# Layer 0 chunk by chunk: one pipeline of normalisation, scan output and router logits, column-tiled projections, and padding written during the dense experts

## The chip, the cores and the metric

One NeuronCore of a Trainium2 chip runs the whole program. The metric is the device time of one launch, in microseconds (us). The core has five engines with a queue each, all in order: TensorE (PE, with its weight loads shown as PEld), VectorE (DVE), ScalarE (ACT), GpSimd (POOL) and SyncE (SP), which here only issues DMAs. They wait for one another through semaphores, written `s_...` below.

## The reference, cut to what matters

Two layers over x of 16 sequences x 256 tokens x 128 features. Each layer has an adaptive layer norm with per-sequence scale and shift, an attention-like part, and a mixture of experts. The change touches layer 0 alone:

```python
h = layernorm(x) * (1 + ca) + sa
delta = sigmoid(h @ W_t.T + b_t) * 0.99 + 0.01      # one number per token
Bu = h @ W_b.T + b_b                                # 16 states per token
_, s = scan(exp(A * delta), Bu)                     # s[t] = a[t] * s[t-1] + Bu[t]
x = x + ga * ((s @ W_c.T + b_c + h * D) @ W_o.T + b_o)
h = layernorm(x) * (1 + cb) + sb
probs = softmax(h @ gate_weight.T)                  # 8 experts, the best two
expert_map = ...    # an expert that is nobody's first choice may be mapped to a similar one
combine = ...       # weight of each expert for each token, through expert_map
x = x + gb * sum_e combine[:, e] * (silu(g_e) * u_e) @ down_e.T    # g_e, u_e = h @ gate_up_e.T
```

Layer 1 (attention with relative positions, then routed experts whose tokens are dispatched by GpSimd) follows and is the same before and after.

## The kernel before

The 4096 tokens are 32 tiles of 128 and 8 chunks (`c`) of 512. `X` holds them in SBUF, `hT` the normalised features with features on partitions. Layer 0 runs as follows, each step in the in-order queues of the engines.

- **SP (from line 418)** loads the modulation weights, the 8 chunks of x, 12 small constants and the tables of layer 1. When the gates are computed (`s_gg`) it stores them and loads them back broadcast (`GATE`). Then it issues the padding: 8 pieces of 2064 KB and one of 903 KB, DRAM to DRAM, which fill the dispatch buffer that layer 1 uses far behind. After `s_yr` (all residuals done) it issues the router's tables (`gateT`, `sim`, `iota`) and the first two experts' weights. These go through the same queue as the padding.
- **Norm 0**: DVE computes `statistics(c)` for all chunks (4 bn_stats and 4 bn_aggr each), ACT one square root over all 32 tiles, DVE one reciprocal, then `normalise` writes `XN` chunk by chunk (4 operations each, double buffered). PE transposes a chunk (4 products with the identity), ACT applies scale and shift into `hT` (2 operations).
- **Projections**: for each half of 8 sequences, 8 products of 256 columns accumulate with the weights `WTpad`, and 8 with `WBpad`. Each is a full-width 128-column weight in which only 16 columns are not zero, shifted by 16 columns per sequence, so the 8 sequences' 16 states stack on the 128 partitions.
- **Scan**: ACT exp, DVE sigmoid and reciprocal, ACT exp, DVE scan, in two halves.
- **Outputs**: PE makes a chunk with 4 pairs of products (lines 1604 and 1605). DVE multiplies by the gate (`gated`, L1019), POOL adds it to X (L655), DVE makes the statistics of the chunk before. The bias row times the gate is added to X ahead of it, by DVE (L1039 and L1043).
- **Norm 1**: the same as norm 0, for all chunks, after all outputs.
- **Router**: PE makes the logits with `hT` as weights, 8 columns moving (L1612, 32 products). DVE and ACT make softmax and the two best of all 32 tiles, PE sums the first choices (L1620), DVE maps the experts, and the weights `WD` come out of a product over 8 x 32 x 8 elements and its reduction (L1140, L1143).
- **Dense experts** (`moe0`): 64 units, expert by expert and chunk by chunk. PE: two up products of 512 columns (L1638, L1639), ACT silu (L794), DVE times (`HM0`, L1170), PE 4 down products (L1627), DVE accumulates with the weight (L1152).

## Time and profile before

| what | us |
|---|---|
| median of 3 runs (lowest, highest) | 982.03 (975.97, 982.88) |
| the profiled execution | 988.27 |
| its span on the core | 986.4 |

Busy time in stages of the span, in us of 20 (granted TensorE clock as a share of full speed):

| stage | PE | DVE | ACT | clock | what runs |
|---|---|---|---|---|---|
| 0 to 20 | 8.40 | 16.63 | 3.12 | 1.00 | loads, statistics, gates |
| 20 to 40 | 15.12 | 17.68 | 9.32 | 1.00 | norm 0, projections; padding issued from 27.15 on |
| 40 to 60 | 16.28 | 13.46 | 3.28 | 0.91 | projections, scan, outputs |
| 60 to 80 | 13.60 | 18.64 | 6.01 | 0.78 | outputs, norm 1 |
| 80 to 100 | 11.82 | 0.53 | 3.67 | 0.59 | wait for a table, logits |
| 100 to 120 | 10.58 | 14.54 | 2.89 | 0.59 | router |
| 120 to 140 | 14.58 | 13.56 | 2.39 | 0.77 | expert weights, dense experts begin |
| 140 to 160 | 20.00 | 12.92 | 4.78 | 1.00 | dense experts |

### The profile page before, as it was taken

How to read it: one execution, taken by the hardware profiler on the slowest of the kernel's cores; microseconds unless marked ns; L12 is line 12 of the kernel's file. 1: busy time of each engine (PE TensorE's matmuls, PEld its weight loads, DVE VectorE, ACT ScalarE, POOL GpSimd, SP SyncE). 2: the span in 40 equal slices, each digit the busy share in tenths (PEclk: the TensorE clock that was granted, in tenths of full speed). 3: DMA queues.
4: the chain of work that ended last, by engine and by line, in shares of the span. 5: the costliest groups of instructions: out<-in, count | busy, mean ns of one | idle time of the engine just before them, and what ended most of it. 6: DMA issues, size and time to landing. Idle time of an engine off the chain costs nothing.

```text
span 986.4 us, 22653 instructions
## 1 busy us (share of the span) xinstructions
PE 837.8 (85%) x8752; PEld 581.6 (59%) x8752; DVE 608.9 (62%) x1652; ACT 354.6 (36%) x670; POOL 246.8 (25%) x248
## 2 busy tenths in 40 slices
PE   3876498999994979999999999998789889999960
PEld 3665355666663544666565665654456678888850
DVE  8882767666687888777877877865346322222218
ACT  1403112122224120563463463563545334444424
POOL 1040000000043640001211211214465624444440
PEclk9985589999997975999999999999799989999985
DMA  8995000000003673214423413312131437777746
GB/s 236 316 321 193 0 2 15 9 9 8 8 0 120 180 215 95 57 27 107 100 32 100 100 28 94 67 30 67 34 84 39 140 100 209 212 220 211 215 126 220
DMA packets 108820, 107.17 MB, mean 109 GB/s; under 512 B 50029, under 2 KB 95022, under 8 KB 108046
## 3 DMA queue, kind: packets, MB, share of 16 engines
q1 hardware_dynamic: 104190, 96.63, 34.9%
q0 software_dynamic: 4544, 9.35, 2.7%
q8 instruction: 60, 0.98, 0.4%
q14 instruction: 26, 0.21, 0.1%
HBM read 80.97 MB, written 44.77 MB: 127 GB/s over the span
## 4 chain that ended last, share of the span: by engine, by line
PE 57%; DVE 19%; issue 10%; SPq 5%; DMA 4%; ACT 2%; POOL 2%; POOLq 0%; DVEq 0%; another core or an unknown queue 0%; ACTq 0%
PE bank L2011 7%; PE bank L1791 7%; PE bank L2021 6%; PE bank L1627 5%; PE bank L1638 5%; PE bank L1639 5%; DVE sb_arena L1259 5%; PE bank L1731 4%; PE bank L1683 4%; PE bank L1709 3%; DMA sb_arena<-in_iota 2%; DVE sb_arena L1249 2%; DVE sb_arena L1251 2%; PE bank L1612 1%; PE bank L1593 1%
## 5 line engine op out<-in xcount | busy, mean ns | idle before, releaser
L1259 DVE TRANSPOSE_TENSOR_REDUCE sb_arena<-bank 128x16 f32<-128x512 f32 x192 | 120.3, 685 | 23.2 <-PE bank L1731 21.8
L837 ACT ACTIVATE sb_arena<-bank 128x512 f32<-128x512 f32 x192 | 99.2, 602 | 50.0 <-PE bank L1731 50.0
L925 ACT ACTIVATE sb_arena<-bank,sb_arena 128x256 f32<-128x256 f32 x156 | 65.3, 471 | 101.7 <-PE bank L2011 100.9
L741 POOL DMA_INDIRECT expert_results<-sb_arena x78 | 74.9, 960 | 94.1 <-DVE sb_arena L1518 77.8
L1627 PEld LDWEIGHTS bank<-sb_arena 128*128 128x128 f32 x512 | 67.5, 194 | 46.5 <-issue 25.7
L794 ACT ACTIVATE sb_arena<-bank 128x512 f32<-128x512 f32 x64 | 38.2, 598 | 152.4 <-PE bank L1639 152.4
L2011 PE MATMUL bank<-sb_arena 128*128 128x256 f32 x312 | 78.7, 396 | 4.6 <-DVE sb_arena L1514 2.1
L1627 PE MATMUL bank<-sb_arena 128*128 128x128 f32 x512 | 69.6, 280 | 14.8 <-DVE sb_arena L1170 14.8
L1791 PE MATMUL bank<-sb_arena 128*16 128x128 f32 x1024 | 72.9, 421 | 5.1 <-issue 4.8
L1170 DVE TENSOR_TENSOR sb_arena<-sb_arena,bank 128x512 f32<-128x512 f32 x64 | 43.7, 685 | 52.7 <-ACT sb_arena L794 52.4
L2021 PE MATMUL bank<-sb_arena 128*128 128x128 f32 x624 | 75.9, 275 | 0.0
L733 POOL DMA_INDIRECT dispatched_rows<-sb_arena x64 | 63.5, 992 | 45.7 <-issue 18.9
L1152 DVE SCALAR_TENSOR_TENSOR sb_arena<-bank,sb_arena 128x128 f32<-128x128 f32 x256 | 71.7, 343 | 3.0 <-PE bank L1627 3.0
L2021 PEld LDWEIGHTS bank<-sb_arena 128*128 128x128 f32 x624 | 72.8, 192 | 0.1
L1638 PE MATMUL bank<-sb_arena 128*128 128x512 f32 x128 | 69.0, 622 | 0.0
L1639 PE MATMUL bank<-sb_arena 128*128 128x512 f32 x128 | 67.5, 609 | 0.0
L2011 PEld LDWEIGHTS bank<-sb_arena 128*128 128x128 f32 x312 | 57.2, 193 | 16.5 <-issue 7.5
L1683 PE MATMUL bank<-sb_arena 128*128 128x56 bf16 (+1 forms) x512 | 62.2, 281 | 5.4 <-DVE sb_arena L1239 3.1
L1249 DVE CAST sb_arena<-bank 128x512 bf16<-128x512 f32 x64 | 43.6, 682 | 37.0 <-PE bank L1683 37.0
L1512 DVE CAST sb_arena<-sb_arena 128x2 uint32<-128x2 f32 x39 | 7.3, 186 | 94.7 <-DMA expert_results<-sb_arena 78.4
L667 POOL TENSOR_TENSOR sb_TMP<-sb_arena,sb_GATE 128x256 f32<-128x256 f32 x16 | 11.3, 726 | 214.4 <-DVE sb_arena L1152 214.3
L1731 PE MATMUL bank<-sb_arena,sb_identb 128*32 128x128 bf16 (+1 forms) x2304 | 62.4, 241 | 0.4 <-DVE sb_arena L1249 0.4
(252 smaller groups left out, 1395.4 us busy)
## 6 DMA issues: line engine op xcount, KB each, us to landing
sb_arena<-in_w SPq DMA_DIRECT2D x39, 578.0 KB
dispatched_rows<-in_padding SPq DMA_DIRECT2D x8, 2064.0 KB, 34.6
sb_arena<-dispatched_rows SPq DMA_DIRECT2D x39, 129.0 KB
sb_GATE<-gates SPq DMA_DIRECT2D x2, 2048.0 KB, 7.0
sb_arena<-q_parts SPq DMA_DIRECT2D x8, 512.0 KB, 5.7
sb_arena<-k_parts SPq DMA_DIRECT2D x8, 512.0 KB, 6.8
context_rel<-sb_arena SPq DMA_DIRECT2D x256, 8.0 KB
sb_arena<-expert_results SPq DMA_DIRECT2D x16, 256.0 KB, 5.8
```

Source lines behind the costliest of these rows:

```text
L741: nc.gpsimd.indirect_dma_start(yD[:, :], bass.IndirectOffsetOnAxis(ap=rid[:, k, r:r + 1], axis=0), YS[:, k, r, :], None).then_inc(s_yo[k], 16)
L837: nc.scalar.activation(dst, src, ACT.Exp).then_inc(s_ex, 1)
L1152: ins = v.scalar_tensor_tensor(out=ACC[:, T, :], in0=src[:, t * D:(t + 1) * D], scalar=wstep[:, (j // NC) % 2, T:T + 1], in1=ACC[:, T, :], ...
L1259: v.tensor_reduce(dst.rearrange("p h b -> p (h b)"), bank[r % RING][:, :].rearrange("p (b c) -> p b c", c=32), AX, ALU.max, apply_transpos ...
L1627: ins = mm(bank[4 + j % 2][:, t * D:(t + 1) * D], HM0[:, j % 2, t * P:(t + 1) * P], W0[:, k, 2 * F0:3 * F0], start=True, stop=True)
L1638: mm(bank[j % 2][:, :], W0[:, k, 0:F0], chunk(hT, c), start=True, stop=True)
L1639: mm(bank[2 + j % 2][:, :], W0[:, k, F0:2 * F0], chunk(hT, c), start=True, stop=True).then_inc(s_up[0], 1)
L1683: ins = mm(out[:, :, :, x], GT4[:, first:first + 32, :].rearrange("p x a -> p (x a)"), queries[:, :, :, q], start=True, stop=True, skip_gr ...
L1731: ins = mm(dst[32 * b:32 * b + 32, :, 32 * b:32 * b + w], identb[:, 32 * a:32 * a + 32], src[:, :, :].rearrange("p (g b) q -> p g b q", g= ...
L1791: ins = mm(out[32 * j:32 * j + 2 * HD, :, x], relk[:, 32 * j + 8 * w + 2 * x:32 * j + 8 * w + 2 * x + 2, :], four, start=True, stop=True, ...
L2011: ins = mm(bank[2 * (k % 2) + b // 2][:, b % 2 * GT:(b % 2 + 1) * GT], W1[:, k, b * P:(b + 1) * P], XT[:, k % 2, :], start=True, stop=True ...
L2021: ins = mm(bank[6 + k % 2][:, r * D:(r + 1) * D], HMT[:, k % 2, b, r * P:(r + 1) * P], W1[:, k, I1 + b * D:I1 + (b + 1) * D], start=(b == ...
```

## The change

- Norm 0 and norm 1 go chunk by chunk: `normalise0(n, c)` on DVE, `deviation` and `features0` on ACT, `transposes0` on PE. Statistics and normalisations of norm 0 alternate on DVE; the gates and masked matrices come after them.
- The 12 constants are one packed load; the loads of x are ordered around it. The router's tables and the first two experts' weights are loaded at the start, into memory of their own.
- Projections: weights of 32 columns, and four products to four groups of 32 output partitions (column tiles). 16 products a half as before.
- Outputs: the bias row is now a product of one row by 512 columns that opens each chunk's accumulation, and DVE's 16 products and 8 additions for it are gone. Behind outputs of chunk c, PE transposes chunk c-2 for norm 1, and DVE does gate product c, statistics c-1 and normalisation c-2.
- Logits: `gateT` (8 columns, widened to 32) is the weight, 512 columns move, four column tiles for four chunks; ACT copies them out and PE transposes them back. The router's DVE steps run on two halves of 16 tiles.
- The expert weights come from two one-hot comparisons over 256 elements each, not from the product over 2048.
- The first two `HM0` products are made ahead of the expert map.
- The padding is issued in pieces behind the experts' weight loads 2 to 7; the SP loop is written out.

```diff
+            for e in range(2, E):
+                sp.wait_ge(s_dn[0], (e - 1) * NC)
+                w0_load(e, e % 2)
+                padding(e - 2)
+                if e >= E - 2:
+                    padding(e)
...
+            def normalise0(n, c):
+                dve.wait_ge(s_sd, n * NC + c + 1)
+                ts = slice(c * TPC, (c + 1) * TPC)
+                link(v.reciprocal(RSTD[:, ts], SD[:, ts]))
+                wait(dve, s_tr, n * NC + c - 1)
+                for t in range(TPC):
+                    T = c * TPC + t
+                    ins = v.tensor_scalar(XN[:, c % 2, t, :], X[:, T, :], MV[:, T, 0:1], RSTD[:, T:T + 1],
+                                          ALU.subtract, ALU.mult)
+                ins.then_inc(s_xn, 1)
...
+            dve.wait_ge(s_gld, 16)
+            for c in range(NC + 2):
+                if c < NC:
+                    dve.wait_ge(s_y, c + 1)
+                    gated(c, bank[4 + c % 2][:, :].rearrange("p (b t f) -> p b t f", b=2, t=2), 0, 0)
+                if 1 <= c <= NC:
                     dve.wait_ge(s_yr, c)
                     statistics(c - 1)
-            dve.wait_ge(s_yr, NC)
-            statistics(NC - 1)
+                if c >= 2:
+                    normalise0(1, c - 2)
...
+            hidden0(0, 0)
+            hidden0(1, 1)
...
+            v.tensor_tensor(EQ[:, :, :], OH1[:, :, :], emaps, ALU.mult)
+            link(v.tensor_tensor(CD[:, :, :], OH2[:, :, :], emaps, ALU.mult))
+            v.tensor_reduce(id1[:, :], EQ[:, :, :], AX, ALU.add)
+            link(v.tensor_reduce(id2[:, :], CD[:, :, :], AX, ALU.add))
+            v.tensor_tensor(EQ[:, :, :], iota_t(NT), bc_e(id1[:, :]), ALU.is_equal)
+            link(v.tensor_tensor(CD[:, :, :], iota_t(NT), bc_e(id2[:, :]), ALU.is_equal))
+            v.tensor_tensor(EQ[:, :, :], EQ[:, :, :], bc_e(w1[:, :]), ALU.mult)
+            link(v.tensor_tensor(CD[:, :, :], CD[:, :, :], bc_e(w2[:, :]), ALU.mult))
+            link(v.tensor_tensor(WD[:, :, :].rearrange("p e t -> p t e"), EQ[:, :, :], CD[:, :, :], ALU.add))
...
+            def projections(h):
                 pe.wait_ge(s_hT, (h + 1) * NC // 2)
-                for pad, at in ((WTpad, S), (WBpad, 0)):
-                    for b in range(8):
-                        ins = mm(bank[2 + h][:, at:at + S], pad[:, 112 - N * b:240 - N * b],
-                                 hT[:, (8 * h + b) * S:(8 * h + b + 1) * S], start=(b == 0), stop=(b == 7))
+                for w, at in ((WT0, S), (WB, 0)):
+                    for x in range(2):
+                        for j in range(4):
+                            b = 8 * h + 2 * j + x
+                            ins = mm(bank[2 + h][32 * j:32 * j + 32, at:at + S], w[:, x, :], hT[:, b * S:(b + 1) * S],
+                                     start=(x == 0), stop=(x == 1), skip_group_check=True)
...
+            def logits0(g):
+                pe.wait_ge(s_hT, NC + 4 * g + 4)
+                for j in range(4):
+                    ins = mm(bank[2 + g][32 * j:32 * j + 32, :], gateT[:, :], chunk(hT, 4 * g + j), start=True, stop=True,
+                             skip_group_check=True)
+                ins.then_inc(s_lt, 1)
...
+            pe.wait_ge(s_zm, 1)
+            for c in range(NC):
+                outputs(c)
+                if c >= 2:
+                    transposes0(1, c - 2)
```

PE, from the last chunk of outputs to the router, before: L1604 and L1605 are the two products of a tile's output, L1580 the transposes, L1612 the logits.

```order
L1604 MATMUL bank<-sb_arena 128x128 [waits s_gt,s_hs]
...
L1605 MATMUL bank<-sb_arena 128x128
L1580 MATMUL bank<-sb_ident,sb_XN 128x128 [waits s_hT,s_xn]
L1580 MATMUL bank<-sb_ident,sb_XN 128x128 x3
...
L1612 MATMUL bank<-sb_arena 128x8 [waits s_hT,s_wm0]
```

PE in the changed kernel, chunk 3 and the beginning of chunk 4: L1663 is the bias row, L1669 and L1670 the output products, L1647 the transposes (of chunks 0 and 1 here).

```order
L1647 MATMUL bank<-sb_ident,sb_XN 128x128 [waits s_gg,s_hT,s_xn]
L1647 MATMUL bank<-sb_ident,sb_XN 128x128 x3
L1663 MATMUL bank<-sb_arena,sb_ones 128x512 [waits s_gt,s_hs]
L1669 MATMUL bank<-sb_arena 128x128
L1670 MATMUL bank<-sb_arena 128x128
...
L1647 MATMUL bank<-sb_ident,sb_XN 128x128 [waits s_hT,s_xn]
L1647 MATMUL bank<-sb_ident,sb_XN 128x128 x3
L1663 MATMUL bank<-sb_arena,sb_ones 128x512 [waits s_gt,s_hs]
```

The transposes, which stood in one block behind all outputs, now stand between the outputs of one chunk and of the next, with their wait for `XN`.

DVE in the outputs, before: L1019 is the gate product, L959 and L962 the statistics.

```order
L1019 TENSOR_TENSOR sb_TMP<-bank,sb_GATE 128x256 [waits s_yr,s_y]
L1019 TENSOR_TENSOR sb_TMP<-bank,sb_GATE 128x256
L959 BN_STATS sb_ST<-sb_X 128x6 [waits s_yr]
L959 BN_STATS sb_ST<-sb_X 128x6 x3
L962 BN_AGGR sb_MV<-sb_ST 128x2 [waits s_dv]
L962 BN_AGGR sb_MV<-sb_ST 128x2 x3
```

DVE in the changed kernel, the iteration of chunk 3: L1074 is the gate product, L985 and L988 the statistics of chunk 2, L997 and L1001 the normalisation of chunk 1; the last row is the gate product of chunk 4.

```order
L1074 TENSOR_TENSOR sb_TMP<-bank,sb_GATE 128x256 [waits s_yr,s_y]
L1074 TENSOR_TENSOR sb_TMP<-bank,sb_GATE 128x256
L985 BN_STATS sb_ST<-sb_X 128x6 [waits s_yr]
L985 BN_STATS sb_ST<-sb_X 128x6 x3
L988 BN_AGGR sb_MV<-sb_ST 128x2 [waits s_dv]
L988 BN_AGGR sb_MV<-sb_ST 128x2 x3
L997 RECIPROCAL sb_RSTD<-sb_SD 128x4 [waits s_sd]
L1001 TENSOR_SCALAR sb_XN<-sb_X,sb_MV,sb_RSTD 128x128 [waits s_tr,s_dv]
L1001 TENSOR_SCALAR sb_XN<-sb_X,sb_MV,sb_RSTD 128x128 x3
L1074 TENSOR_TENSOR sb_TMP<-bank,sb_GATE 128x256 [waits s_yr,s_y]
```

A reciprocal and four normalising operations have come in ahead of the next gate product.

## Rows read from the trace of the kernel before

**Rows 1.** Timeline, ACT and DVE: start, us, engine, line, out<-in, [idle before <-releaser].
```profile
82.67 1.28 ACT L786 ACT_TABLE_LOAD   x1
103.71 0.42 DVE L1084 TENSOR_REDUCE sb_arena<-bank 128x32 f32<-128x256 f32 x1 [23.19 <-PE bank L1612]
127.53 1.12 DVE L1152 SCALAR_TENSOR_TENSOR sb_arena<-bank,sb_arena 128x128 f32<-128x128 f32 x4 [1.57 <-PE bank L1627]
149.64 1.12 DVE L1152 SCALAR_TENSOR_TENSOR sb_arena<-bank,sb_arena 128x128 f32<-128x128 f32 x4
```

**Rows 2.** The chain of waits, 0 to 130: start us, us, what.
```profile
33.00 13.83 PE bank L1593 x64
70.22 19.52 DMA sb_arena<-in_iota
118.26 3.85 DVE sb_arena L1140
122.13 2.30 DVE sb_arena L1143
```

**Rows 3.** Timeline, from the start to the first output.
```profile
5.64 0.48 DVE L967 MEMSET bank<- 128x512 f32 x1 [0.18 <-DVE bank L967]
17.10 0.36 DVE L980 COPY sb_MOD<-bank 128x192 f32<-128x192 f32 x1
20.55 2.14 DVE L997 TENSOR_SCALAR sb_arena<-bank,sb_arena 128x128 f32<-128x128 f32 x8
47.37 0.30 DVE L1047 TENSOR_SCALAR sb_arena<-sb_arena 128x256 f32<-128x256 f32 x1 [2.50 <-ACT sb_arena L777]
49.37 0.39 DVE L1050 TENSOR_SCALAR sb_arena<-bank,sb_arena 128x256 f32<-128x256 f32 x1
50.53 0.71 PE L1604 MATMUL bank<-sb_arena 128*128 128x128 f32 x2 [3.72 <-DVE sb_arena L1052]
```

**Rows 4.** Timeline, DVE and PE while outputs run.
```profile
63.59 0.72 DVE L1019 TENSOR_TENSOR sb_TMP<-bank,sb_GATE 128x256 f32<-128x256 f32 x2
65.42 0.72 DVE L1019 TENSOR_TENSOR sb_TMP<-bank,sb_GATE 128x256 f32<-128x256 f32 x2
65.89 0.39 PE L1605 MATMUL bank<-sb_arena 128*128 128x128 f32 x2
66.11 0.39 PE L1604 MATMUL bank<-sb_arena 128*128 128x128 f32 x2
```

**Rows 5.** Timeline, transposes of one chunk, and DVE's last two chunks of norm 1.
```profile
31.32 0.66 PE L1580 MATMUL bank<-sb_ident,sb_XN 128*128 128x128 f32 x4 [0.59 <-DVE sb_XN L1007]
78.39 2.14 DVE L1007 TENSOR_SCALAR sb_XN<-sb_X,sb_MV,sb_RSTD 128x128 f32<-128x128 f32 x8 [0.18 <-PE bank L1580]
```

**Rows 6.** Timeline, PE, layer 1's column-tiled products (four of 256, then four of 128).
```profile
443.16 0.60 PE L1763 MATMUL bank<-sb_arena 128*9 128x256 f32 x8
443.59 0.39 PE L1767 MATMUL bank<-sb_arena 128*9 128x128 f32 x8
```

**Rows 7.** Timeline, PE, f32 products of 512 columns in the dense experts.
```profile
133.44 1.02 PE L1638 MATMUL bank<-sb_arena 128*128 128x512 f32 x2
134.30 1.02 PE L1639 MATMUL bank<-sb_arena 128*128 128x512 f32 x2
...
136.05 1.02 PE L1638 MATMUL bank<-sb_arena 128*128 128x512 f32 x2
```

**Rows 8.** Stages, PE: stretch, us, busy (records), granted clock, DMA share, GB/s.
```profile
50.00:52.00 2.00, 1.47 (x7) 0.66 0.66 220
...
78.00:80.00 2.00, 1.82 (x8) 0.50 1.03 352
80.00:82.00 2.00, 1.60 (x8) 0.66 1.06 352
```

**Rows 9.** DMA issues, 0 to 120 and 110 to 310: count, KB each, us to landing.
```profile
sb_arena<-in_w SPq DMA_DIRECT2D x2, 192.0 KB, 18.7
...
sb_arena<-in_w SPq DMA_DIRECT2D x6, 192.0 KB, 2.3
```

## Prediction: what the change does to the time, and why

> **What bounds the kernel now.** I read the 20 us stages first, then the chain of waits of the first 130 us, then the timelines of PE and DVE in it. From the dense experts on, the program stays as it is; what is changed lies ahead of the first weighted sum of an expert, at 127.53 [rows 1]. Up to there one engine after another works alone. The reader should see three long pieces in the chain [rows 2]: 13.83 us of scan projections on PE, 19.52 us until the last small router table lands behind the padding, and two big DVE operations of 3.85 and 2.30 us that make the expert weights. After 127.53 PE is the bound, at 2.61 us a unit (133.44 to 136.05) [rows 7]; the eighth accumulation later starts at 149.64 [rows 1]. So the sum is made for that instant: whatever the changed kernel has gained or lost there is its gain or loss. The padding has to be complete only for the dispatch, far behind.
>
> **Start until the first scan output.** Before, DVE makes all statistics, then everything else, and the first output product starts at 50.53 [rows 3]. Now DVE interleaves statistics and normalisation, and its own work is the bound: clearing the banks until 6.1, eight statistics of 1.19 (1.83 for gate product and statistics together, less 0.64 for the product) [rows 3, 4] = 9.5; eight normalisations of 1.07 [rows 5] and 0.3 for a reciprocal and its wait (a value that I choose, as the operand is eight times smaller than before) = 11.0; modulations and gate arithmetic 3.45; the masked matrices 2.14, with the widened bias row, the cast and the product M2 about 1.2 more; two sigmoids of 2.0; shift and scan 1.16 [rows 3]. That is 38.6; I take 39.0 for small waits. The two halves of projections go from 16 products in a row to groups of four column tiles. PE then has the second half ready at about 31, long before DVE asks at 34.5. The nearest rows are the attention's column tiles: four f32 products of 256 columns take 0.43 us together [rows 6], so a half costs 1.7 instead of 6.9. The worst case is that they do not overlap: 6.9 a half, which ends the second half near 41 and puts the outputs at 47 to 48. I take the overlap, since the row is of the same width and type. **Gain 11.5.**
>
> The Trainium skill (TensorE: Matmul & The Clock Gate, Part 3) says that a weight load overlaps running products only when the row group differs, and gives 2.38 times for three column tiles. By it the two halves would cost about 6 us (an estimate), still hidden under DVE's work, and the sum would not move by more than a microsecond.
>
> **The output pipeline, where I expect most of the gain to go.** Before, outputs, gate products and statistics run freely, and all normalisations follow; the last one ends at 80.53 [rows 5], 30.0 after the first output. Now look at the two orders in the section on the change. PE does outputs(c), then the transposes of chunk c-2, then outputs(c+1). Those transposes wait for DVE's normalisation of chunk c-2, which stands last in DVE's iteration c; and DVE's iteration c+1 begins with the gate product, which waits for outputs(c+1). So from chunk 3 on, the two engines alternate: five periods, each the DVE part plus the PE part. DVE: 0.64 + 1.19 + 0.3 + 1.07 = 3.2. PE at the high clock: transposes 0.46 (four, from the 0.66 that includes the drain [rows 5]), the bias row as one product of 512 columns 0.86 [rows 7], eight products of 0.22 = 1.77 [rows 4], and 0.2 until DVE sees it: 3.3. At the low clock about twice that, 6.5. A product with one input row is not shorter, as time goes with the moving columns; nothing in the rows gives a reason to price it lower.
>
> Outside the five periods stand three outputs (2.8 + 2.6 + 2.6, high), one DVE part of 3.2 and a tail on DVE of one statistics and two normalisations, 3.9. High throughout: 8.0 + 3.2 + 5 x 6.5 + 3.9 = 47.6. Low throughout, 24.3 of PE work more: 71.9. Which clock? Before the outputs of the old kernel PE idled 3.72 us [rows 3] and the granted clock was at its low level when they began (0.66 in the stage 50 to 52, where 0.50 is 1.2 GHz and 1.00 is 2.4 GHz) [rows 8]. In the new loop every burst follows 3.2 us of idleness, close to that. Once low, a burst lasts 6.3 us, of which the second half is full products; they may bring the clock back, and the next idle stretch takes it away. I take half of the PE work low: 47.6 + 12.2 = 59.8. **Loss 59.8 - 30.0 = 29.8.**
>
> **From the last normalisation to the router.** Before: 80.53 to 103.71 [rows 1, 5], 23.2 us: transposes, the wait for the table [rows 2], 32 products whose moving side has 8 columns. The tables are now loaded at the start and the padding leaves the queue, so nothing lands late. After the last normalisation there remain: transposes 0.9, features about 1.0, four column tiles of 512 columns 0.9 to 1.7, a copy 0.6, the table load 1.28 [rows 1] and an exponential 0.3, some 5.9; the low half's shift is done by then. **Gain 17.3.**
>
> **The router and the weights.** Before, 23.8 from 103.71 to 127.53 [rows 1]. Now the same steps run on two halves of the tiles. An operation of 256 elements takes 0.42 and 0.04 to the next; of 128 elements I take 0.33 in all (an eighth of a microsecond fewer columns; the fixed part stays). Behind the first exponential: 8 + 2 + 7 + 8 + 7 operations of 0.33 = 10.6, the count 0.55, five small ones 1.0, the two hidden products that moved ahead 1.3, twelve small ones of the expert map 3.0, nine operations of 0.42 to 0.46 in place of the two big ones = 4.0, the copy 0.2: 20.7. **Gain 3.1.** Splitting gains little, since most of an operation's time is fixed; the gain is 6.15 less 4.0, and that PE's first product is no longer waited for.
>
> **The lead of two units.** The first two hidden products now run before the expert map, so PE has two down products and two further up products done when DVE starts to accumulate: 2 x 2.61 = 5.2, less the 1.9 that PE then waits for DVE's first turns, less some 1.3 for PE starting this stage low as before. **Gain 2.0.**
>
> **Padding in the experts.** 16.5 MB leave the stretch 27 to 90 and go out one or two pieces behind each weight load, when before only the weights were in flight. A weight load behind the padding landed after 18.7 us, alone after 2.3 [rows 9]. Now each weight load is issued ahead of its padding, 21 us before it is needed, and the padding behind the previous one (nine pieces took some 60 us together until 89.74 [rows 2], so about 7 us a piece, at most two) is gone by then. Cost 0; if that cover failed, PE would wait up to 16 us once an expert.
>
> **Sum.** -11.5 + 29.8 - 17.3 - 3.1 - 2.0 = **-4.1 us**. The profiled execution took 988.27 us with a span of 986.4; the median of the three runs is 982.03. I subtract from the median: **978**.
>
> **Rivals.**
> - *The clock stays high in the loop* (idle stretches of 3.2 are a little shorter than the 3.72 that went low): 12.2 less, -16.3, **966**. Chance 0.17.
> - *The clock stays low in the whole loop*: 12.2 more, +8.1, **990**, slower than before. For it: in the stage 78 to 80, PE was busy 1.82 of 2.00 with transposes and stayed at 0.50 [rows 8]; the loop's bursts begin with transposes and a product of one row. It decides for slower once more than two thirds of the loop's PE work is low. Chance 0.22. The Trainium skill (the same page, Part 4) states that transposes do not bring the clock up; here it rose within 80 to 82 (0.66) with nothing but transposes before it [rows 8], so the rule is not exact, but it points this way.
> - *The column tiles do not overlap*: the outputs start 8 later, 986. Chance 0.04.
> - *Padding disturbs the experts* (code loads or weights late at a loop's start): one to two microseconds an expert, 982 to 990. Chance 0.05.
> - *The forecast*, a mixed clock with the alternation: 970 to 986. Chance 0.52.
>
> **The numbers.** Range 966 to 990: it takes in both clock cases' centres and leaves about a fifth outside, for their far halves and the other rivals. About 1% is what a measurement of this kernel can tell from no change, 9.8 us. Faster by more: most of the high clock case and a small part of the mixed one, 0.23. Slower by more: the far end of the low case and of the padding case, 0.11. Within: 0.66.
>
> **What would show it.** In the changed kernel's timeline: the first output product near 39; then DVE gate products 6.5 apart at a high clock, up to 9.8 at a low one, with DVE idle behind PE's outputs and PE idle behind XN in turn. If the gate products come 3.5 apart, the alternation is wrong and the kernel is 15 to 20 us faster. The projections should take about 2 us a half, the logits no wait on a table, and the first accumulation should stand near 124 to 128 with the eighth later near 145. Weight loads that land after 2 to 3 us show that the padding costs nothing. If the stages behind the experts differ by more than two or three microseconds, I have overlooked something there.

## The result and the profile after

| | before | after |
|---|---|---|
| median of the runs beside each other | 980.48 us (4 runs, 975.97 to 982.88) | 986.63 us (4 runs, 984.55 to 995.11) |
| ratio after to before, 95% interval | | 1.0095 (1.0056 to 1.0133) |
| profiled execution, its span | 988.27, 986.4 us | 984.55, 982.7 us |

The change made the kernel about 1% slower; 4.1 us faster were forecast. Here and below, ratios leave out executions of the slow state (longer, at a lower clock), while the medians are of all executions. The two profiled executions stand the other way round: that of before was slow for its kernel, that of after the fastest of its four. So the spans can't be subtracted. What can be is an instant ahead of the part in which single executions differ (more on that at the end): the last weighted sum of the dense experts was at 301.32 before and is at 309.86 now, 8.5 us later, and 980.48 x 1.0095 is 9.3 us more.

The changed kernel in the 20 us stages (stretch, us, then busy us and records of PE, PEld, DVE, ACT and POOL, granted clock of PE, DMA share, GB/s):

```profile
40.00:60.00 20.00, 16.20 (x60) 10.91 (x60) 7.22 (x30) 1.89 (x4) 3.79 (x3) 0.69 0.46 176
60.00:80.00 20.00, 13.50 (x46) 8.97 (x44) 6.17 (x30) 2.41 (x6) 2.52 (x2) 0.67 0.00 1
80.00:100.00 20.00, 13.49 (x45) 9.41 (x44) 6.18 (x30) 2.41 (x6) 2.53 (x2) 0.50 0.00 0
100.00:120.00 20.00, 14.87 (x61) 8.53 (x60) 9.49 (x44) 7.21 (x14) 1.26 (x1) 0.69 0.00 1
```

From 60 to 100 PE is busy for 27 of 40 us and DVE for 12.35 of 40, together nearly the whole 40; the timeline below shows that they work in turn, not at the same time. The clock is at 0.50, its level of 1.2 GHz, for all of the third stage. One period of that loop, in the timelines of DVE and PE (start, us, engine and line, operation, output<-inputs, count; in brackets the idle time ahead of it and who ended it):

```profile
74.58 0.76 DVE L1074 TENSOR_TENSOR sb_TMP<-bank,sb_GATE 128x256 f32<-128x256 f32 x2 [6.79 <-PE bank L1670]
76.62 1.11 DVE L1001 TENSOR_SCALAR sb_XN<-sb_X,sb_MV,sb_RSTD 128x128 f32<-128x128 f32 x4
77.80 0.70 PE L1647 MATMUL bank<-sb_ident,sb_XN 128*128 128x128 f32 x4 [3.25 <-DVE sb_XN L1001]
78.42 2.07 PE L1663 MATMUL bank<-sb_arena,sb_ones 1*128 1x512 f32 x2
80.42 0.80 PE L1669 MATMUL bank<-sb_arena 128*128 128x128 f32 x2
...
84.25 0.76 DVE L1074 TENSOR_TENSOR sb_TMP<-bank,sb_GATE 128x256 f32<-128x256 f32 x2 [6.51 <-PE bank L1670]
...
94.33 0.76 DVE L1074 TENSOR_TENSOR sb_TMP<-bank,sb_GATE 128x256 f32<-128x256 f32 x2 [6.92 <-PE bank L1670]
...
104.41 0.76 DVE L1074 TENSOR_TENSOR sb_TMP<-bank,sb_GATE 128x256 f32<-128x256 f32 x2 [6.92 <-PE bank L1670]
```

PE idles 3.25 for DVE's XN, then DVE idles 6.5 to 6.9 for PE's products; gate products stand 9.7 to 10.1 apart. In that burst the bias row (1x512) takes 2.00 until the next product starts. Before, gate products stood 1.83 apart [rows 4].

The 0.67 of 60 to 80 does not mean that part of the products ran fast. In stretches of 2 us (same columns as the stages above):

```profile
62.00:64.00 2.00, 2.00 (x12) 2.00 (x11) 0.00 (x0) 0.00 (x0) 0.00 (x0) 0.50 0.00 0
64.00:66.00 2.00, 0.60 (x3) 0.30 (x2) 1.37 (x6) 0.00 (x0) 0.53 (x1) 0.84 0.00 0
66.00:68.00 2.00, 0.15 (x1) 0.15 (x2) 1.72 (x10) 1.20 (x3) 0.73 (x1) 1.00 0.00 0
68.00:70.00 2.00, 2.00 (x6) 0.92 (x5) 0.00 (x0) 0.00 (x0) 0.00 (x0) 0.51 0.00 0
```

PE's products end at 64.6 and its next burst starts at 67.85. The clock was high in just that pause, and low again for the products. The output products of all five bursts of the loop ran at the low clock, 0.43 apart where they stood 0.22 apart before.

The other pieces of the changed stretch, in the same view, and two rows of its DMA issues (count, KB each, median us to landing):

```profile
33.59 1.93 PE L1656 MATMUL bank<-sb_arena 128*32 128x256 f32 x32 [1.58 <-ACT sb_arena L772]
...
40.55 1.86 PE L1663 MATMUL bank<-sb_arena,sb_ones 1*128 1x512 f32 x2 [5.02 <-DVE sb_arena L1095]
...
110.09 1.12 DVE L1001 TENSOR_SCALAR sb_XN<-sb_X,sb_MV,sb_RSTD 128x128 f32<-128x128 f32 x4
...
117.44 0.28 DVE L1135 TENSOR_REDUCE sb_arena<-sb_arena 128x16 f32<-128x128 f32 x1 [4.22 <-ACT sb_arena L810]
...
137.48 1.13 DVE L1210 SCALAR_TENSOR_TENSOR sb_arena<-bank,sb_arena 128x128 f32<-128x128 f32 x4
...
158.13 1.12 DVE L1210 SCALAR_TENSOR_TENSOR sb_arena<-bank,sb_arena 128x128 f32<-128x128 f32 x4
...
309.86 1.09 DVE L1210 SCALAR_TENSOR_TENSOR sb_arena<-bank,sb_arena 128x128 f32<-128x128 f32 x4
...
dispatched_rows<-in_padding SPq DMA_DIRECT2D x8, 2064.0 KB, 10.2
...
sb_arena<-in_w SPq DMA_DIRECT2D x8, 192.0 KB, 2.4
```

With these rows the forecast's sum can be set against the trace, term by term (all in us):

| piece | forecast | before | after | difference |
|---|---|---|---|---|
| start to first output product | -11.5 | 50.53 | 40.55 | -10.0 |
| first output to last XN | **+29.8** | 30.0 | 70.7 | **+40.7** |
| last XN to router (second half's exponential used) | -17.3 | 23.2 | 6.2 | -17.0 |
| router to first weighted sum | -3.1 | 23.8 | 20.0 | -3.8 |
| first to ninth weighted sum | -2.0 | 22.1 | 20.65 | -1.5 |
| sum | -4.1 | | | +8.4 |

One term missed. The four others are within 1.5 us each, and the padding, forecast at 0, is read from the two rows of the DMA issues: weights land after 2.4 us, and the experts take 172.4 us (137.48 to 309.86) against 173.8 before; the difference of 1.4 is that of the first nine (-1.5, the last row), and nothing is left for the padding.

### The profile page after: what moved, and what is told of

Read it like the earlier page. It is cut to its first block, busy times and chain, and to the rows that moved or that the text cites. A ratio compares the mean times of both kernels' runs of the same rounds, so it can differ in the third digit from the quotient of the medians.

```text
span 982.7 us, 22603 instructions
## 1 busy us (share of the span) xinstructions
PE 834.4 (85%) x8726; PEld 569.5 (58%) x8726; DVE 601.5 (61%) x1661; ACT 359.3 (37%) x687; POOL 246.3 (25%) x244
## 4 chain that ended last, share of the span: by engine, by line
PE 56%; DVE 20%; POOL 8%; DMA 6%; issue 6%; ACT 3%; SPq 2%; POOLq 0%; DVEq 0%
PE bank L2101 6%; PE bank L2111 6%; PE bank L1881 6%; POOL dispatched_rows L723 6%; PE bank L1715 5%; PE bank L1726 5%; PE bank L1727 5%; DVE sb_arena L1316 5%; PE bank L1821 4%; PE bank L1773 4%; PE bank L1799 3%; DMA dispatched_rows<-sb_arena 2%; DVE sb_arena L1306 2%; DMA expert_results<-sb_arena 2%; DVE sb_arena L1308 2%
## 5 line engine op out<-in xcount | busy, mean ns | idle before, releaser
L1316 DVE TRANSPOSE_TENSOR_REDUCE sb_arena<-bank 128x16 f32<-128x512 f32 x192 | 120.3, 684 | 23.8 <-PE bank L1821 22.3
L1881 PE MATMUL bank<-sb_arena 128*16 128x128 f32 x1024 | 68.4, 423 | 0.0
L1726 PE MATMUL bank<-sb_arena 128*128 128x512 f32 x128 | 67.6, 611 | 0.0
L1727 PE MATMUL bank<-sb_arena 128*128 128x512 f32 x128 | 65.7, 595 | 0.0
L1799 PE MATMUL bank<-sb_arena 32*128 32x256 bf16 x512 | 52.9, 285 | 6.5 <-DVE sb_arena L1316 4.5
```

The source lines that it names most:

```text
L1316: v.tensor_reduce(dst.rearrange("p h b -> p (h b)"), bank[r % RING][:, :].rearrange("p (b c) -> p b c", c=32), AX, ALU.max, apply_transpos ...
L1726: mm(bank[j % 2][:, :], W0[:, k, 0:F0], chunk(hT, c), start=True, stop=True)
L1727: mm(bank[2 + j % 2][:, :], W0[:, k, F0:2 * F0], chunk(hT, c), start=True, stop=True).then_inc(s_up[0], 1)
L1799: mm(dst[:, x * S:(x + 1) * S], KG[k][rows, g, 0:P], QG[k][rows, g, :], start=(x == 0), stop=False, skip_group_check=True)
L1881: ins = mm(out[32 * j:32 * j + 2 * HD, :, x], relk[:, 32 * j + 8 * w + 2 * x:32 * j + 8 * w + 2 * x + 2, :], four, start=True, stop=True, ...
```

## The experiments

Three theories of the 40.7 us were tested; they don't exclude one another. **A**: the place of the transposes in PE's order makes PE and DVE wait in turn. **B**: the bias row is a cost of its own. **C**: the clock is low because of something in that loop, and what that is. Every ratio is to the kernel before on the same chip, which took 980.4 us in e1 to e4, 1001.9 in e5 to e8 (another chip, on which the kernel before took 2% longer), and 980.2 in the last four (e9, e10, e11 and the changed kernel again). So times of different groups are compared by ratio. The changed kernel again, beside e9, e10 and e11, the second run of e1:

> The changed kernel itself once more, on the same chip as the other kernels of this call, so that they can be set against it directly. As before: ratio to the kernel before 1.006 to 1.013, last normalisation ending near 111, first accumulation near 137.

It took 988.83 (8 runs), ratio 1.0091 (1.0059 to 1.0123), with the last XN ending at 108.9 and the first weighted sum at 135.57.

**e1: products ahead of the transposes.**

```diff
             for c in range(NC):
                 outputs(c)
-                if c >= 2:
-                    transposes0(1, c - 2)
+                if c >= 3:
+                    transposes0(1, c - 3)
+            transposes0(1, 5)
```

> The changed kernel, in which TensorE issues the transposes of chunk c-3 behind the outputs of chunk c, where it was those of chunk c-2; those of chunk 5 follow the loop. Nothing else is changed. In the changed kernel the gate products stand 9.7 to 10.1 us apart from chunk 3 on (6.8 of PE, then 3.15 of DVE). Theory A (PE and DVE wait for each other in turn): the outputs of the next chunk now run while DVE normalises, so a period is the longer of the two and not their sum. With the clock still low it is some 6.8 us, 16 to 20 us less in all, 967 to 971 against the 986.6 of the changed kernel; with PE busy without a pause the clock may rise as well, a period is then DVE's 3.2 to 3.6, and the time 950 to 958. Theory B (the order costs nothing; the stage is long because one bias row and twelve other PE instructions a chunk at a low clock are that long): period unchanged, 984 to 988.

The median is 952.46 us, the ratio 0.970 (0.9669 to 0.9731). That is theory A, with both of its parts: the waiting in turn is gone and the clock is up. DVE in the loop:

```profile
62.29 0.76 DVE L1074 TENSOR_TENSOR sb_TMP<-bank,sb_GATE 128x256 f32<-128x256 f32 x2 [0.71 <-PE bank L1670]
...
65.75 0.76 DVE L1074 TENSOR_TENSOR sb_TMP<-bank,sb_GATE 128x256 f32<-128x256 f32 x2 [0.31 <-PE bank L1670]
...
69.23 0.75 DVE L1074 TENSOR_TENSOR sb_TMP<-bank,sb_GATE 128x256 f32<-128x256 f32 x2 [0.31 <-PE bank L1670]
...
105.21 1.12 DVE L1210 SCALAR_TENSOR_TENSOR sb_arena<-bank,sb_arena 128x128 f32<-128x128 f32 x4
```

DVE waits 0.3 us where it waited 6.9, the period is 3.47, and the first weighted sum comes 32 us earlier than in the changed kernel. One place in the order of one engine is worth 3.9% of the time, the difference between 1.0095 and 0.970. Once more, on the chip of the last group:

> The kernel of e1 once more on the same chip as the changed kernel and the candidate. As before: ratio to the kernel before 0.967 to 0.973, and to the changed kernel 0.958 to 0.964, which is the price of one line's order in the program (transposes of c-2 instead of c-3).

The median is 951.42, the ratio 0.9713 (0.9669 to 0.9757), and 0.962 of the changed kernel's 988.83.

**e2: the second normalisation behind all outputs again** (its loops on DVE, PE and ACT follow the output loop; the deviations stay one to a chunk).

```diff
             for c in range(NC):
                 outputs(c)
-                if c >= 2:
-                    transposes0(1, c - 2)
+            for c in range(6):
+                transposes0(1, c)
...
-                if c >= 2:
-                    normalise0(1, c - 2)
+            for c in range(NC):
+                normalise0(1, c)
```

> The changed kernel with one part undone: the second normalisation again stands behind all eight outputs on DVE and PE (the deviations stay one to a chunk, the logits stay as changed). Theory A: without the alternation the outputs run at 2.6 us a chunk as before the change plus 0.9 to 2.0 for the bias row, 28 to 37 us for eight, then 11 us of normalisations; the last one ends at 80 to 89 where the changed kernel had 111.2, so 22 to 31 us less, 956 to 965. Theory B (the bias row and the low clock alone make the stage long): the outputs need 6.5 us a chunk here too, the normalisations come on top, and the time is within 3 us of the changed kernel's 986.6 or above.

The median is 959.15, the ratio 0.9798 (0.9755 to 0.9841). Theory A again: without the interleaving, all other parts of the change together gain 2%. But the stretch from the first output to the last XN is 42.9 us (41.12 to 84.06), and 30.0 before. The rows of DVE show why:

```profile
58.64 0.75 DVE L1074 TENSOR_TENSOR sb_TMP<-bank,sb_GATE 128x256 f32<-128x256 f32 x2 [1.08 <-PE bank L1670]
...
61.67 0.76 DVE L1074 TENSOR_TENSOR sb_TMP<-bank,sb_GATE 128x256 f32<-128x256 f32 x2 [1.09 <-PE bank L1670]
```

A chunk takes 3.03 at the high clock, with DVE waiting 1.09 for PE. Before, it was 1.83 without a wait: with the bias row PE is the bound.

**e5: e2 without the bias row.** The output bias of layer 0 is missing from its result.

```diff
-                mm(bank[4 + c % 2][:, :], ones[0:1, :], crow[0:1, :], start=True, stop=False, skip_group_check=True)
...
-                    mm(dst, HSC[:, b // 8, at:at + P], ZM[:, b % 8, :], start=False, stop=False, skip_group_check=True)
+                    mm(dst, HSC[:, b // 8, at:at + P], ZM[:, b % 8, :], start=True, stop=False, skip_group_check=True)
```

> The kernel of e2 (second normalisation behind the outputs, 959.2 us) without the bias row: the product of ones and the bias is left out, and with it the output bias of layer 0 is missing from the result. In e2 the gate products stood 3.03 us apart with the clock up (PE the bound: 1.05 for the bias row to the next product, eight products of 0.22, 0.2 more) and 5.6 apart in the first two chunks at the low clock; the kernel before had 1.83 (DVE the bound) and no such row. If the bias row is what the stage pays for, periods fall to 1.83 to 1.95 and the first two chunks by 2.0 each: 9 to 11 us less, 948 to 950. If it lies beside DVE's work, as a cover of 1.1 us of DVE waiting would suggest at first sight, 1 us less a chunk at most and the time is 955 to 959.

The median is 970.26, the ratio 0.9696 (0.9625 to 0.9767); e2 had 0.9798. The point estimates differ by 1.0%, 10 us, as theory B says, though the intervals overlap; the trace is clearer:

```profile
44.16 0.76 DVE L1074 TENSOR_TENSOR sb_TMP<-bank,sb_GATE 128x256 f32<-128x256 f32 x2 [2.60 <-PE bank L1669]
46.07 0.76 DVE L1074 TENSOR_TENSOR sb_TMP<-bank,sb_GATE 128x256 f32<-128x256 f32 x2 [1.16 <-PE bank L1669]
...
55.27 0.72 DVE L1074 TENSOR_TENSOR sb_TMP<-bank,sb_GATE 128x256 f32<-128x256 f32 x2
```

The period is DVE's 1.83 again, and the last XN ends at 70.35, 13.7 us ahead of e2. That is more than eight bias rows at the high clock cost beyond DVE's cover (8 x 1.20 = 9.6): the first two gate products stand 1.9 apart, and 5.6 in e2. PE starts at the low clock in both; here it is up when the second chunk's products begin (0.91 in 44 to 46), in e2 only at 52.

**e3: the idle stretch filled.**

```diff
                 if c >= 2:
+                    for x in range(2):
+                        mm(bank[7][:, :], M2[:, :], wmod[:, 0, 0:CH], start=True, stop=True)
                     transposes0(1, c - 2)
```

> The changed kernel with two products of 512 columns added into each idle stretch of PE in the output loop (behind the outputs of chunk c, ahead of the transposes that wait for DVE; their result is not used), so that PE is busy where it idled 3.15 us a period. It tells what the clock adds to the alternation. If the idle stretches are what keeps the clock low, the granted clock goes up, PE's burst falls from 6.8 to about 3.4, the period from 9.9 to 6.5, and the time by 15 to 20 us to 967 to 972. If the clock stays low whatever stands in the gap, the two products take 3.5 to 4.0 us, a little more than the idle time, and the time goes up by 2 to 6 us, to 989 to 993.

The median is 971.46, the ratio 0.9903 (0.9867 to 0.9939). A stage of PE's clock and two gate products:

```profile
80.00:100.00 20.00, 14.85 (x82) 7.92 (x80) 10.30 (x50) 6.20 (x15) 2.53 (x2) 1.00 0.00 1
...
69.35 0.76 DVE L1074 TENSOR_TENSOR sb_TMP<-bank,sb_GATE 128x256 f32<-128x256 f32 x2 [3.78 <-PE bank L1670]
...
76.29 0.76 DVE L1074 TENSOR_TENSOR sb_TMP<-bank,sb_GATE 128x256 f32<-128x256 f32 x2 [3.78 <-PE bank L1670]
```

With 12 products of no use added, the first weighted sum is at 122.22, 15 us ahead of the changed kernel's (the ratios make it 19). The clock is at 1.00 where it was at 0.50, and the period 6.94. The alternation is all there still, now at the high clock: this splits the loss. The stretch from first output to last XN is 55.9 here (41.08 to 96.98), 70.7 in the changed kernel, 38.6 in e1: some 15 us of the 40.7 are the clock, 17 the waiting in turn at the high clock, and the rest of about 9, which e1 has too, is put down to the bias rows and the low start; e10 below, which changes those, is back at 31.2.

**e4: the bias row in the idle stretch.**

```diff
+            def bias_row(c):
+                wait(pe, s_gt, c - 1)
+                mm(bank[4 + c % 2][:, :], ones[0:1, :], crow[0:1, :], start=True, stop=False, skip_group_check=True)
...
-                wait(pe, s_gt, c - 1)
-                mm(bank[4 + c % 2][:, :], ones[0:1, :], crow[0:1, :], start=True, stop=False, skip_group_check=True)
...
+            bias_row(0)
             for c in range(NC):
                 outputs(c)
+                if c < NC - 1:
+                    bias_row(c + 1)
                 if c >= 2:
                     transposes0(1, c - 2)
```

> The changed kernel with the bias row of chunk c+1 issued behind the outputs of chunk c, ahead of the transposes that wait for DVE: the alternation stays, but the one-row product of 512 columns (2.0 us at the low clock in the trace) lies in PE's idle time. By its own duration alone a period falls by 2.0, from 9.9 to 7.9, seven periods, 12 to 14 us less: 973 to 975. If PE's shorter idle stretch also lets the clock rise, up to 25 us less, 962. If the bias row is hidden already, no change: 985 to 988.

The median is 963.79, the ratio 0.9836 (0.9798 to 0.9873), a gain of more than the 12 to 14 us of the row's own duration:

```profile
58.06 0.76 DVE L1074 TENSOR_TENSOR sb_TMP<-bank,sb_GATE 128x256 f32<-128x256 f32 x2 [3.69 <-PE bank L1672]
...
65.84 0.76 DVE L1074 TENSOR_TENSOR sb_TMP<-bank,sb_GATE 128x256 f32<-128x256 f32 x2 [4.62 <-PE bank L1672]
...
80.28 0.76 DVE L1074 TENSOR_TENSOR sb_TMP<-bank,sb_GATE 128x256 f32<-128x256 f32 x2 [3.94 <-PE bank L1672]
...
60.00:80.00 20.00, 14.35 (x65) 12.32 (x64) 7.36 (x36) 3.62 (x9) 2.69 (x3) 0.69 0.00 1
```

Periods are 6.8 to 7.8 with the clock still mixed. The trace up to the first weighted sum accounts for 16.2 us (121.31 against 137.48); the ratios, 1.0095 and 0.9836, make 25. The other 9 lie behind the first weighted sum and are not explained.

**e9: the bias over 128 input rows.** What, other than idle time, holds the clock?

```diff
+            nc.gpsimd.memset(crow[:, :], 0.0).then_inc(s_set, 1)
...
+            dve.wait_ge(s_set, 2)
             v.tensor_tensor(crow[0:1, :].rearrange("p (t d) -> p t d", t=TPC),
...
-                mm(bank[4 + c % 2][:, :], ones[0:1, :], crow[0:1, :], start=True, stop=False, skip_group_check=True)
+                mm(bank[4 + c % 2][:, :], ones[:, :], crow[:, :], start=True, stop=False, skip_group_check=True)
```

> The changed kernel with its bias product over all 128 input rows in place of one (the bias in row 0, zeros in the others, set once at the start), the same 512 columns; nothing else. In e1, PE was busy 2.00 of 2.00 us from 42 to 52 and the granted clock stayed at 0.50; in e5, the same outputs without the one-row products, it rose within the first chunk (first gate product 3.6 us after the first output product, the second 1.9 later). If the one-row product is part of what keeps the clock low, the clock now rises in the later half of each burst: the first two chunks together 3 to 4 us shorter, the periods of 9.9 to 10.1 fall to 8.5 to 9.2, and the time by 8 to 11 us (976 to 979 where the kernel before has 980, a ratio to the kernel before of 0.995 to 0.999). If rows don't matter and only idle time does, every period stays at 9.7 to 10.1, and the ratio that of the changed kernel, 1.009.

The median is 970.15, the ratio 0.9884 (0.9831 to 0.9938). The same order, the same products and columns, one small memset more, and 18.7 us less than the changed kernel beside it (988.83). Up to the first weighted sum the two traces account for 13.5 of that (122.06 against 135.57); the rest lies behind it and is not explained. e1, stretches of 2 us:

```profile
44.00:46.00 2.00, 2.00 (x11) 2.00 (x11) 0.00 (x0) 0.00 (x0) 0.00 (x0) 0.50 0.00 0
46.00:48.00 2.00, 2.00 (x6) 0.92 (x4) 0.76 (x2) 0.00 (x0) 0.34 (x1) 0.50 1.48 462
48.00:50.00 2.00, 2.00 (x7) 1.35 (x7) 0.00 (x0) 0.00 (x0) 0.92 (x1) 0.50 0.00 0
50.00:52.00 2.00, 2.00 (x11) 2.00 (x10) 0.00 (x0) 0.00 (x0) 0.00 (x0) 0.50 0.00 0
```

e9, the same stretches, and two gate products of its loop:

```profile
44.00:46.00 2.00, 2.00 (x13) 1.76 (x13) 0.27 (x1) 0.00 (x0) 0.00 (x0) 0.81 0.18 66
46.00:48.00 2.00, 2.00 (x18) 1.76 (x16) 0.49 (x2) 0.00 (x0) 1.27 (x1) 1.00 1.48 462
...
73.66 0.76 DVE L1076 TENSOR_TENSOR sb_TMP<-bank,sb_GATE 128x256 f32<-128x256 f32 x2 [3.40 <-PE bank L1672]
...
80.22 0.76 DVE L1076 TENSOR_TENSOR sb_TMP<-bank,sb_GATE 128x256 f32<-128x256 f32 x2 [3.40 <-PE bank L1672]
```

Both start an output burst after 5.02 us of idleness, near 41. With the one-row product PE is busy without a gap and the clock is still at its low level at 52; with 128 rows it is up after 44.

This first burst alone would not settle it. The changed kernel's second trace has the one-row products and the same start, and its clock is up at 46:

```profile
46.00:48.00 2.00, 2.00 (x10) 1.12 (x10) 0.76 (x2) 0.00 (x0) 0.42 (x1) 0.97 1.28 462
...
46.74 0.76 DVE L1074 TENSOR_TENSOR sb_TMP<-bank,sb_GATE 128x256 f32<-128x256 f32 x2 [4.54 <-PE bank L1670]
...
49.70 0.76 DVE L1074 TENSOR_TENSOR sb_TMP<-bank,sb_GATE 128x256 f32<-128x256 f32 x2 [2.21 <-PE bank L1670]
```

From the first output product to the rise it took 10 to 11 us in the six other traces that start with a one-row product behind 5.02 us of idleness (the changed kernel, e1, e2, e3, e7, e11), 4.9 in this one, and under 4 in the two without one-row products (e5, e9). So the long low start goes with the one-row product in most executions, not in all.

In the loop the difference is plainer: e9's periods are 6.56 to 9.29 instead of 9.4 to 10.1 (both traces of the changed kernel), although PE idles 3.25 us in each, and the clock is 0.91 in 60 to 80 and 0.74 in 80 to 100, where the changed kernel beside it has 0.59 and 0.50. So the one-row product was counted too cheaply twice: 2.0 us for itself, and products behind it that stay at the low clock. It is not the only cause: e3 keeps the one-row product and has 1.00 in both stages, and e1 too gets there from its third chunk on and keeps it, as PE has hardly a pause there. Theory C holds in that form: full products in the gap or a full bias product lift the clock. What exactly the chip counts was not tested, nor whether a product of another length would do the same.

**e6: the start filled, and the load order.**

```diff
-            load_x(0)
             sp.dma_start(cT[:, :, :], A["cT"]).then_inc(s_cw, 16)
             sp.dma_start(wmod[:, :, :], A["wmod"]).then_inc(s_cw, 16)
+            load_x(0)
...
+                if c >= 2:
+                    bias_row(c)
...
+            for x in range(2):
+                mm(bank[7][:, :], ident[:, :], wmod[:, 0, 0:CH], start=True, stop=True)
             pe.wait_ge(s_zm, 1)
+            bias_row(0)
+            bias_row(1)
...
```

> The kernel of e1 (952.5 us) with three small edits: two products of 512 columns whose result is not used and the bias rows of chunks 0 and 1 are issued ahead of the wait for the first scan, where PE idled 5.02 us; and the modulation weights are loaded ahead of the first rows of x. If it is the idle stretch that makes the outputs begin at the low clock, the first two gate products, which stood 5.5 us apart and 4.9 of waiting behind the first product, come 3 us apart and 4 to 6 us are gained; the load order gives 1 more as DVE waited 1.25 for the modulations. 945 to 949. If the clock stays low whatever is ahead, only the two bias rows (4.1 us at the low clock, of which 2 on the path) are hidden: 949 to 951. If the filling comes late and pushes the outputs back, 953 to 956.

The median is 964.56, the ratio 0.965 (0.9566 to 0.9734), where e1 had 0.970; the intervals overlap, and the three edits were not run apart. The trace shows the step: the first gate products are at 42.38 and 44.78 (46.82 and 52.31 in e1), the first weighted sum at 97.20 (105.21). DVE's wait for PE's first transposes, which stand behind the modulation products, is 0.46 instead of the 1.66 of e1's second run.

**e10: the candidate**, e1 with the load order and the early bias rows of e6 and the 128 rows of e9, and without products of no use.

```diff
...
+            bias_row(0)
+            bias_row(1)
             for c in range(NC):
                 outputs(c)
-                if c >= 2:
-                    transposes0(1, c - 2)
+                if c >= 3:
+                    transposes0(1, c - 3)
+            transposes0(1, 5)
```

> The products-ahead order of e1, the modulation weights ahead of the first rows of x, the bias rows of chunks 0 and 1 ahead of the wait for the first scan, and all bias products over 128 input rows; no product without use. It is the version that I would put in place of both kernels. e1 had a ratio of 0.970 to the kernel before, e6 (with two products of no use instead of the full rows) 0.965. If the rows matter for the clock, the outputs start high or rise within the first chunk, the last normalisation ends at 71 to 72 as in e6 (79.5 in e1), first accumulation at 97, ratio 0.962 to 0.966. If not, the first two chunks run at the low clock and about 3 us are lost: first accumulation at 100 to 102, ratio 0.966 to 0.969.

The median is 941.67, the ratio 0.9636 (0.9583 to 0.9689). By its point estimate it is the fastest of all, though its interval overlaps those of e1 and e6. On the same chip its median is 39 us below the kernel before, 47 below the changed one and 10 below e11.

```profile
39.26 0.49 PE L1675 MATMUL bank<-sb_arena 128*128 128x128 f32 x2 [3.02 <-DVE sb_arena L1097]
...
69.30 1.11 DVE L1002 TENSOR_SCALAR sb_XN<-sb_X,sb_MV,sb_RSTD 128x128 f32<-128x128 f32 x4
...
96.07 1.13 DVE L1212 SCALAR_TENSOR_TENSOR sb_arena<-bank,sb_arena 128x128 f32<-128x128 f32 x4
```

First output to last XN takes 31.2 here (the first two bias rows lie ahead of it), close to the 30.0 before, but with most of the second normalisation's transposes and features done inside it.

**e8 and e7: the padding.** e8 is the kernel before with the padding moved into the experts and nothing else; e7 is the changed kernel with its padding at the start. The edit of e8:

```diff
-            for e in range(E):
+            def padding(e):
                 sp.dma_start(xsD[e * TOK:(e + 1) * TOK, :].rearrange("(k r) n -> k (r n)", r=GT),
...
+            for e in range(2, E):
+                sp.wait_ge(s_dn[0], (e - 1) * NC)
+                w0_load(e, e % 2)
+                padding(e - 2)
+                if e >= E - 2:
+                    padding(e)
```

> The kernel before with one part of the change alone: the eight pieces of padding go out during the dense experts, one or two behind each expert's weights. In its trace PE's 32 router products began at 89.78, 8.2 us after the last transposes, because the last small table landed behind the padding; without it they can begin at about 82.8. So 7.0 less: 973 to 975, down to 970 if the clock, no longer idle for 8 us, is up for some of the 32 products. If another thing was late too (the old start, the weights), 977 to 981. If padding in the experts costs time there, the gain shrinks by that, visible as a longer way from the first accumulation to the end of the experts (173.8 us before).

The median is 991.81, the ratio 0.9907 (0.9868 to 0.9947), 9.3 us of the 1001.9 on that chip. PE's router products before:

```profile
89.78 10.41 PE L1612 MATMUL bank<-sb_arena 128*128 128x8 f32 x48 [8.18 <-DMA sb_arena<-in_iota]
```

The same in e8, and the instants behind them:

```profile
80.69 12.87 PE L1613 MATMUL bank<-sb_arena 128*128 128x8 f32 x64
...
93.67 0.42 DVE L1085 TENSOR_REDUCE sb_arena<-bank 128x32 f32<-128x256 f32 x1 [13.53 <-PE bank L1613]
...
117.50 1.13 DVE L1153 SCALAR_TENSOR_TENSOR sb_arena<-bank,sb_arena 128x128 f32<-128x128 f32 x4 [1.57 <-PE bank L1628]
```

They start at 80.69 instead of 89.78, and the router at 93.67 instead of 103.71 [rows 1]: 10.0 us, from one move in SP's queue. The wait of 8.18 for the small table is gone. From the first to the last weighted sum it is 173.8 us, as before, so the padding costs the experts nothing. It is 10 of the 17 us of the forecast's third term.

> The changed kernel with its eight pieces of padding sent at the start again, behind the gates, and none during the dense experts; router tables and the first two experts' weights stay ahead of them in the queue. By my ledger the place of the padding costs nothing in the experts (each weight load landed after 2.4 us), so this is as the changed kernel, 984 to 988. If the padding disturbs the experts by some way that the landing times don't show, the time falls by 4 or more, to 982 or less. If the traffic disturbs the output loop (gates of DVE late, small loads late), it rises above 990.

The median is 1012.89, the ratio 1.0138 (1.0078 to 1.0198), against 1.0095 of the changed kernel; the intervals overlap. Up to the last weighted sum its trace is 2 us ahead of the changed kernel's, at 307.74, and its loop is the same (periods of 9.7 to 10.1). That the place of the padding doesn't matter once the tables are ahead of it is consistent with this; a gain or loss under 1% isn't excluded.

## Why the prediction was wrong

**Bound and order of the argument: right.** The alternation was read out of the two orders before anything ran, it is what the trace shows, and e1 and e2, which take it away in two ways, gain 39 and 29 us on the changed kernel by their ratios. Its DVE part was forecast as 3.2 (3.25 of PE waiting in the trace).

**The step that failed is "Which clock?"** The text took half of the PE work at the low level, 59.8 us for the stretch; it was 70.7, next to the 71.9 of the case "low throughout". The term is 10.9 of the 12.5 us between -4.1 and +8.4; about 2 of the 10.9 are the bias rows' own length (below), the rest is mostly the clock. The step in its words: "they may bring the clock back, and the next idle stretch takes it away". In the trace no burst of the loop brought it back for its own output products; it came up behind the burst that ended at 64.6, in the pause, where it was worth next to nothing. The rival "the clock stays low in the whole loop" had 990 and a chance of 0.22; the runs gave 986.6 to 988.8. Of what was said for it, the runs bear out the pauses (e3) and the product of one row (e9). The transposes are not shown to matter: e3 has them in the same place, at 1.00. That its 71.9 comes so near to 70.7 is partly luck: the first three chunks took 14.0 (40.55 to 54.55) and not 16.0, as the third ran at the high clock, and the five bursts 33.8 and not 32.5. The half was a middle between two cases and not the reading of a row. The one row at hand, 1.82 of 2.00 busy at 0.50 [rows 8], spoke for the low case, and was spent on its chance, not on the forecast. The row 50 to 52 was read loosely, too: its 0.66 is a mean, by which the clock was still high until 50.64, and the first output product started at 50.53.

**The bias row was mis-sized.** The text gave it 0.86 at the high and 1.71 at the low clock. It measured 1.05 (e1, 62.62 to 63.67) and 2.0. The reading "time goes with the columns" held for its own duration, nearly (0.86 with 128 rows), but not for what it did to the products behind it: e9 gains 18.7 us, of which about eight times 0.19 are its own duration. It also makes PE the bound of the outputs where DVE was (e2 against e5: 3.03 and 1.83 a chunk); the sum had that, at 2.6 a chunk.

**Start: right, a little short.** 38.6 was the sum of DVE's work and 39.0 forecast; 40.55 came. DVE waited 1.40 us for the second chunk of x and 1.25 for PE's first transposes behind the modulation products; e6 shows the latter as the price of loading x ahead of the modulation weights. The column tiles overlap as the attention's did: 32 records in 1.93 us. The first half took 3.30, most of it at the low clock. By what the Trainium skill says on weight loads and column tiles (TensorE: Matmul & The Clock Gate, Part 3) the two halves would have cost about 6 us (an estimate). They took 5.2 together, half of it at the low clock; two at the high clock would be 3.9, and the measurement decides.

**Last XN to router, router, lead, padding: right.** -17.3, -3.1, -2.0 and 0 against -17.0, -3.8, -1.5 and 0. e8 shows the third term's larger part by itself. The parts of the router's gain were not run apart.

**Range and chances.** 966 to 990 holds 986.6, and 1.0095 is just within 1%, but the interval of the ratio leaves no change out and the sign was the other one; that the range holds it is the merit of the low rival, not of the forecast. The low case, with its centre at +8.1, deserved the largest chance of the clock cases and not 0.22.

The Trainium skill (same page, Part 1, HAM oscillation) describes a loop whose pause takes the clock down in every iteration, so that each burst pays for the climb, and advises to reorder the loop so that PE has no pause. e1 is that remedy, and the runs agree with it (0.970), though most of its gain is the waiting in turn that went with it; e3, which fills the pause alone, has 1.00 where the changed kernel had 0.50.

## What to carry to other kernels

Interleaving two chains saves time only if, on each engine, the instruction that waits for the slower partner stands behind the work that the partner needs next. Write the two orders side by side, and if each engine's wait is released by the last item of the other's iteration, the period is the sum of both; one chunk more of lag makes it the larger of the two. Where such a loop leaves PE short pauses, count its work at the low clock until a row shows otherwise, and give a broadcast or bias product all its input rows: it cost one memset here.

## What was not expected of the hardware

- A product with one input row and 512 columns takes 1.05 us at the high and 2.0 at the low clock until the next product starts, where one with 128 rows takes 0.86 (e9, 45.47 to 46.33) and 1.84 (e9, 40.85 to 42.69). More input is cheaper.
- With one-row products among full ones, the granted clock stayed at 0.50 for ten microseconds (42 to 52 in e1) in which PE was busy for 2.00 of each 2.00; with 128 rows it was at 0.81 in 44 to 46 and 1.00 from 46 to 54. In one of seven traces with the one-row product it rose after 4.9 us all the same.
- The mean clock of a stage says little about the products in it: 0.67 in 60 to 80 of the changed kernel, with every output product of the loop at the low level and the high level in the pauses.
- Behind the experts, single executions of the same code differ: from the last weighted sum to the end it took 685.1 us in the profiled execution before, 672.8 after, 677.2 in e1, 667.1 in e4. The difference lies mostly behind the attention, in the dispatch and the second experts: up to the first dispatching DMA these four traces agree within 3.4 us, and behind it they need 289.4 to 305.8. The forecast called more than two or three microseconds there a sign of an oversight; an instant ahead of it (8.5 us later) and the ratio (9.3) agree without it. What causes it was not tested; it is why terms were read from instants ahead of it, and the verdict from medians.
